# A graph network of four layers on one core: keys loaded and counted first, key and value products inside the first edge sort, zero fill in two halves

## The reference

```python
edge_index = jnp.stack([src, dst])
x = _layernorm(x + _L0(x, edge_index, edge_attr_32, Wq, Wk, Wv, We))
x = _layernorm(x + _L1(x, src, dst, kernel, bias))
x = _layernorm(x + _L2(x, edge_attr_64, edge_index, W_node, W_edge, a_node, a_edge))
x = _layernorm(x + _L3(x, node_vec, W_homo, b_homo, W_hete, b_hete, W_self, b_self, src, dst))

# _L0: attention over the edges into each node, 8 heads of 16
scores = einsum('ehc,ehc->eh', q[dst], k[src]) / sqrt(16) + edge_attr @ We.T
alpha = segment_softmax(scores, dst)
out = segment_sum(v[src] * alpha, dst)
```

## Time and profile before

| | us |
|---|---|
| time, median of 3 runs | 3610.65 (3607.81 to 3611.58) |
| time of the profiled execution | 3604.32 |
| span of the profiled execution | 3602.3 |
| TensorE busy | 1759.1 (49%) |
| VectorE busy | 2287.1 (63%) |
| ScalarE busy | 831.7 (23%) |
| GpSimd busy | 1605.7 (45%) |
| mean granted TensorE clock | 0.704 |

### The profile page before, as it was taken

The page is one execution under the profiler, slowest core; times in us unless marked ns, Lnnn a source line. Parts: engine busy times, 40 slices in busy tenths (PEclk is TensorE's granted clock), DMA queues, the critical chain, the costliest instruction groups (busy, mean ns, idle before and its releaser), DMA issues. The chain is left out here.

```text
span 3602.3 us, 41432 instructions
## 1 busy us (share of the span) xinstructions
PE 1759.1 (49%) x11225; PEld 1197.1 (33%) x11225; DVE 2287.1 (63%) x4545; ACT 831.7 (23%) x2162; POOL 1605.7 (45%) x1514
## 2 busy tenths in 40 slices
PE   2301110103256565539971455249301889984994
PEld 1200000002133333327761345224201227863663
DVE  6974444428866666568977555340485995665987
ACT  0220000002222222214541000000101884542331
POOL 0027777730177777717756577600484003530000
PEclk7555555555576767569985787579655999985997
DMA  1944444470588778787740455338094655641861
GB/s 33 412 132 106 105 104 106 105 52 3 161 236 237 234 237 235 224 60 137 159 89 1 100 109 109 40 124 303 31 390 151 234 182 108 129 88 58 223 186 44
DMA packets 685207, 520.38 MB, mean 144 GB/s; under 512 B 396219, under 2 KB 641677, under 8 KB 670935
## 3 DMA queue, kind: packets, MB, share of 16 engines
q1 hardware_dynamic: 626245, 415.27, 45.8%
q0 software_dynamic: 58752, 102.49, 8.2%
HBM read 356.87 MB, written 160.71 MB: 144 GB/s over the span
## 5 line engine op out<-in xcount | busy, mean ns | idle before, releaser
L654 POOL DMA_INDIRECT table<-pay_own,stage x432 | 420.9, 974 | 571.1 <-ACT q L672 237.5
L971 POOL DMA_INDIRECT adjacency<-gm_slot,slot_tmp x440 | 480.6, 1092 | 225.7 <-issue 134.1
L654 POOL DMA_INDIRECT table<-q,stage x424 | 412.2, 972 | 129.2 <-issue 121.9
L633 PE MATMUL banks<-work,acc 128*128 128x52 bf16 x856 | 98.8, 216 | 757.2 <-DVE acc L620 666.0
L633 PEld LDWEIGHTS banks<-work,acc 128*128 128x128 bf16 x856 | 75.1, 116 | 812.6 <-DVE acc L612 561.2
L715 PE MATMUL banks<-pool,both 128*128 x1320 | 269.0, 377 | 25.2 <-issue 20.7
L1981 POOL TENSOR_TENSOR pool<-pool,raw 128x260 f32<-128x260 f32 x110 | 115.1, 1046 | 355.1 <-DMA pool<-table 246.0
L610 DVE TENSOR_SCALAR acc<-acc,pidx 128x512 bf16<-128x512 bf16 x214 | 80.6, 377 | 285.1 <-DMA acc<-low_rows_by_src 277.4
L612 DVE SCALAR_TENSOR_TENSOR acc<-acc,raw,after 128x128 bf16<-128x128 bf16 x856 | 243.0, 344 | 0.0
L1186 PE MATMUL banks<-both,pool 128*128 128x128 f32 x880 | 157.4, 342 | 131.5 <-DVE both L1517 131.4
L715 PEld LDWEIGHTS banks<-pool,both 128*128 128x128 bf16 x1320 | 163.9, 124 | 100.3 <-issue 42.2
(11 more groups left out here) (462 smaller groups left out, 4413.3 us busy)
## 6 DMA issues: line engine op xcount, KB each, us to landing
work<-adjacency SPq DMA_DIRECT2D x75, 1600.0 KB, 6.7
adjacency<-slots SPq DMA_DIRECT2D x30, 1320.0 KB, 33.0
acc<-table SPq DMA_DIRECT2D x110, 332.0 KB
pool<-table SPq DMA_DIRECT2D x110, 256.0 KB
pool<-table SPq DMA_DIRECT2D x220, 128.0 KB, 2.4
work<-adjacency SPq DMA_DIRECT2D x25, 832.0 KB, 5.4
work<-adjacency SPq DMA_DIRECT2D x25, 768.0 KB, 5.0
acc<-low_rows_by_dst SPq DMA_DIRECT2D x110, 128.0 KB, 4.4
```

What stands on the lines that cost most here:

```text
L633: nc.tensor.matmul(to, rohT_keys[k % 2][:, j, :], pairs[o][:, :, bass.ds(n * G + j, 1), :] .rearrange("p h t s -> p h (t s)"), start=True, ...
L654: nc.gpsimd.indirect_dma_start(to, bass.IndirectOffsetOnAxis(ap=stage[k][:, j:j + 1], axis=0), pay[k][:, j, 0:width], None).then_inc(lande ...
L971: nc.gpsimd.indirect_dma_start(adjacency, bass.IndirectOffsetOnAxis(ap=pair_at[:, t:t + 1], axis=0), pair_n[:, t:t + 1], None).then_inc(co ...
```

## The change

- The two edge key arrays are loaded ahead of the node features, ahead of SyncE's wait for the clearing of `xs`, and VectorE splits them in the start block. The block no longer waits for the weights; TensorE does, ahead of its first transpose in the first sort.
- The key and value products and their split go into the first sort as seven more entries of its pipeline (`key_value_parts`), with work at every fourth step, one block of nodes at a time. ACT makes the high and the middle part, VectorE the two subtractions.
- The folding of the attention vectors, and the split of the node vector (25 columns), go into the block between the sorts.
- The zero fill is cut in two: 16 pieces in the first counting as before, and the remaining 15, with the two fills of 440 KB, in the block between the sorts, behind the five number loads on SyncE's stream. The wait for them moves to `slot_ids`.

```diff
@@ -272,11 +272,14 @@
-        s_w, s_c, s_cd, s_wp = sem("weights_loaded"), sem("iotas_ready"), sem("consts_chain"), sem("wfold_done")
-        s_xz = sem("x_cleared")
+        s_w, s_c, s_xz = sem("weights_loaded"), sem("iotas_ready"), sem("x_cleared")
+        s_kl, s_kc = sem("keys_loaded"), sem("keys_chain")
+        ints = [slot_tmp[k][:, 0:ET].bitcast(I32) for k in range(4)]
         with nc.Block() as block:
...
             def _(sp):
+                for k in range(2):
+                    sp.dma_start(ints[k], keys[k]).then_inc(s_kl, 16)
                 sp.wait_ge(s_xz, 1)
@@ -299,7 +302,6 @@
...
                     sp.dma_start(b3[:, j, :], L3_b[j:j + 1, :].to_broadcast([P, D])).then_inc(s_w, 16)
-                sp.wait_ge(s_w, 16 * 21)
@@ -327,21 +329,15 @@
...
                 nc.vector.tensor_scalar(pidx[:, :], diff[:, 0:1], -1.0, None, ALU.mult)
-                ch = Chain(v, s_cd)
-                v.wait_ge(s_w, 16 * 21)
-                ch.link(nc.vector.tensor_copy(a_rep, avec[:, 3:4].to_broadcast([FE64, P])))
-                v.wait_ge(s_wp, 2)
-                nc.vector.tensor_copy(wge[:, :], ps[0][:, 0:FE64])
-
-                nc.vector.tensor_copy(wn[:, 64:65], ps[1][:, 1:2])
-                nc.vector.tensor_copy(wn[:, 65:66], ps[1][:, 0:1])
-                nc.vector.tensor_copy(wn[:, 66:67], ps[1][:, 2:3])
-
-            @block.tensor
-            def _(pe):
-                pe.wait_ge(s_cd, 1)
-                nc.tensor.matmul(ps[0][:, 0:FE64], a_rep, wedge[:, :], start=True, stop=True).then_inc(s_wp, 1)
-                nc.tensor.matmul(ps[1][:, 0:4], wnode[:, :], avec[:, :], start=True, stop=True).then_inc(s_wp, 1)
+                ch = Chain(v, s_kc)
+                v.wait_ge(s_kl, 32)
+                for k in range(2):
+                    ch.link(nc.vector.tensor_scalar(ints[2 + k], ints[k], 7, None, ALU.arith_shift_right))
+                    ch.link(nc.vector.tensor_scalar(ints[k], ints[k], P - 1, None, ALU.bitwise_and))
+                for k in range(2):
+                    nc.vector.tensor_copy(raw[:, 2 * k, 0:ET], ints[k])
+                    nc.vector.tensor_scalar(raw[:, 2 * k + 1, 0:ET], ints[2 + k], 1.0, None, ALU.add)
+                nc.vector.memset(work[:, 0:NH * (ET + 1)].rearrange("p (h t) -> p h t", h=NH)[:, :, 0:1], 0.0)
@@ -855,6 +851,7 @@
...
                     ch = Chain(v, s_sl)
+                    v.wait_ge(s_az, 16 * CLEARS)
                     tmp = slot_tmp[0][:, :]
@@ -1310,54 +1307,85 @@
-        node_products("kv", lambda b: xs[:, b, :], 2 * D, wqkv[:, D:3 * D], take_kv)
-        s_kp, s_kl, s_kc = sem("kv_parts"), sem("keys_loaded"), sem("keys_chain")
-        ints = [slot_tmp[k][:, 0:ET].bitcast(I32) for k in range(4)]
-        with nc.Block() as block:
-            @block.sync
-            def _(sp):
-                for k in range(2):
-                    sp.dma_start(ints[k], keys[k]).then_inc(s_kl, 16)
-
-            @block.vector
-            def _(v):
-                split16(Chain(v, s_kp).link, kv_rest, [kv16[:, :, k, :] for k in range(3)])
-                ch = Chain(v, s_kc)
-                v.wait_ge(s_kl, 32)
-                for k in range(2):
-                    ch.link(nc.vector.tensor_scalar(ints[2 + k], ints[k], 7, None, ALU.arith_shift_right))
-                    ch.link(nc.vector.tensor_scalar(ints[k], ints[k], P - 1, None, ALU.bitwise_and))
-                for k in range(2):
-                    nc.vector.tensor_copy(raw[:, 2 * k, 0:ET], ints[k])
-                    nc.vector.tensor_scalar(raw[:, 2 * k + 1, 0:ET], ints[2 + k], 1.0, None, ALU.add)
-                nc.vector.memset(table["src"][:, :, 0:1], 0.0)
+        def key_value_parts():
+
+            s_t, s_c, s_p, s_h, s_r, s_m, s_l = (sem(f"kv_{k}") for k in (
+                "turned", "turned_copied", "product", "high_kept", "rest_left", "middle_kept", "low_kept"))
+            rest = [own_row[k][:, :, :].rearrange("p g n -> p (g n)").bitcast(F32) for k in range(2)]
+            product = ps[1][:, 0:2 * D]
+
+            def each_block(todo):
+                return lambda eng, n, k: todo(eng, n // 4) if n % 4 == 0 and n // 4 < NB else None
+
+            def turn(pe, b):
+                if b == 0:
+                    pe.wait_ge(s_w, 16 * 21)
+                wait(pe, s_c, b)
+                nc.tensor.transpose(ps[0][:, 0:P], xs[:, b, :], ident[:, :]).then_inc(s_t, 1)
+
+            def copy(act, b):
+                act.wait_ge(s_t, b + 1)
+                wait(act, s_p, b - 1)
+                nc.scalar.copy(xt[:, b % 2, :], ps[0][:, 0:P]).then_inc(s_c, 1)
+
+            def multiply(pe, b):
+                pe.wait_ge(s_c, b + 1)
+                wait(pe, s_r, b)
+                nc.tensor.matmul(product, xt[:, b % 2, :], wqkv[:, D:3 * D], start=True, stop=True).then_inc(s_p, 1)
+
+            def high(act, b):
+                act.wait_ge(s_p, b + 1)
+                nc.scalar.copy(kv16[:, b, 0, 1:KVW], product).then_inc(s_h, 1)
+
+            def left(v, b):
+                v.wait_ge(s_h, b + 1)
+                wait(v, s_l, b - 1)
+                nc.vector.tensor_tensor(rest[b % 2], product, kv16[:, b, 0, 1:KVW], ALU.subtract).then_inc(s_r, 1)
+
+            def middle(act, b):
+                act.wait_ge(s_r, b + 1)
+                nc.scalar.copy(kv16[:, b, 1, 1:KVW], rest[b % 2]).then_inc(s_m, 1)
+
+            def low(v, b):
+                v.wait_ge(s_m, b + 1)
+                nc.vector.tensor_tensor(kv16[:, b, 2, 1:KVW], rest[b % 2], kv16[:, b, 1, 1:KVW], ALU.subtract).then_inc(s_l, 1)
+
+            return {"tensor": [(2, each_block(multiply)), (0, each_block(turn))],
+                    "scalar": [(5, each_block(middle)), (3, each_block(high)), (1, each_block(copy))],
+                    "vector": [(6, each_block(low)), (4, each_block(left))]}
+
         s_az = lasting_sem("adjacency_cleared")
-        def clear_adjacency(sp):
+        def clear_fills(sp):
...
                              slots[:, 0:2, :].rearrange("p k t -> p (k t)")).then_inc(s_az, 16)
+
+        def clear_adjacency(sp, first, last):
+
             cells = adjacency[0:CELLS, :].rearrange("(p n) o -> p (n o)", p=P)
-            for c in range(CLEARS - 2):
+            for c in range(first, last):
                 n = min(6 * T, CELLS // P - c * 6 * T)
...
         counting = histogram("src")
-        counting["sync"] = {"begin": clear_adjacency, "step": [lambda sp, i: None], "steps": ET // (2 * G)}
+        counting["sync"] = {"begin": lambda sp: clear_adjacency(sp, 0, CLEARS // 2), "step": [lambda sp, i: None], "steps": ET // (2 * G)}
         run((counting, 0, ET // (2 * G), 1))
...
         loads, parts, ready = own_rows()
-        run((stepwise("src", together(placing, parts, scatter_rows("src", loads, table1, ROW1, ready, placing["placed"])),
+        run((stepwise("src", together(placing, parts, scatter_rows("src", loads, table1, ROW1, ready, placing["placed"]),
+                                      key_value_parts()),
                       cleared), 0, ET // (4 * G), 1), lead=T)
...
         s_rb = [sem(f"sorted_ids_loaded{c}") for c in range(5)]
+        s_cd, s_wp = sem("fold_chain"), sem("fold_products")
         back = pay_own[:, :, :, :].rearrange("p k g n -> p (k g n)")[:, 0:4 * T].rearrange("p (t c) -> p t c", c=4)
@@ -1367,11 +1395,29 @@
...
                                      .rearrange("(t p) c -> p t c", p=P)).then_inc(s_rb[c], 16)
+                clear_adjacency(sp, CLEARS // 2, CLEARS - 2)
+                clear_fills(sp)
...
             def _(v):
-                v.wait_ge(s_az, 16 * CLEARS)
                 nc.vector.memset(table["dst"][:, :, 0:1], 0.0)
+                ch = Chain(v, s_cd)
+                ch.link(nc.vector.tensor_copy(a_rep, avec[:, 3:4].to_broadcast([FE64, P])))
+                rest = small[:, 0, 0:NB]
+                ch.link(nc.vector.tensor_copy(rest, nv[:, :]))
+                split16(ch.link, rest, [kv16[:, :, k, 0] for k in range(3)])
+                v.wait_ge(s_wp, 2)
+                nc.vector.tensor_copy(wge[:, :], ps[0][:, 0:FE64])
+
+                nc.vector.tensor_copy(wn[:, 64:65], ps[1][:, 1:2])
+                nc.vector.tensor_copy(wn[:, 65:66], ps[1][:, 0:1])
+                nc.vector.tensor_copy(wn[:, 66:67], ps[1][:, 2:3])
+
+            @block.tensor
+            def _(pe):
+                pe.wait_ge(s_cd, 1)
+                nc.tensor.matmul(ps[0][:, 0:FE64], a_rep, wedge[:, :], start=True, stop=True).then_inc(s_wp, 1)
+                nc.tensor.matmul(ps[1][:, 0:4], wnode[:, :], avec[:, :], start=True, stop=True).then_inc(s_wp, 1)
         counting = histogram("dst")
```

## The result

| | before | changed |
|---|---|---|
| time, median (range), 4 runs each | 3609.23 us (3606.98 to 3611.58) | 3580.34 us (3573.31 to 3582.76) |
| ratio to before, 95% interval | | 0.9917 (0.990 to 0.9934) |
| span of the profiled execution | 3602.3 us | 3571.5 us |
| mean granted TensorE clock | 0.704 | 0.832 |
| counting starts | 89.92 us | 30.51 us |

The kernel got 28.9 us faster, 0.8%. From the page of the changed kernel: the span, busy times, and two rows of the 40 slices, the granted clock and the DMA share. The clock is at 0.9 and above in the first ten slices, 893 us, where it was 0.50 in counting and first sort before.

A forecast was written before the change was run, and what follows sets the result against it. No one engine bounds the kernel: a plain sequence at the start, then VectorE (counting), GpSimd (first sort), SyncE's issues between the sorts. -59.9 + 1 + 0 + 30.4 = -28.5 us gives 3582 us, range 3568 to 3602.

The forecast's parts named there:

- part 1: Start, products and split: keys load early, the block no longer waits for weights, counting starts at 30.06 instead of 89.92: -59.9 us.
- part 2: Products and split inside the first sort: waits are covered, only VectorE's operations slow GpSimd's scatters a little: +1 us.
- part 3: Fold and small split between the sorts: about 3 us of work hidden under VectorE's 26.10 idle us: 0.
- part 4: Second half of the fill between the sorts: the block ends with SyncE's last issue, 827.8 instead of 797.42: +30.4 us.
- slower: Rival, first sort: the new stages' chain of ACT and VectorE uses up the lead, GpSimd waits: 127 us, 3709; chance 0.04.
- lock: Rival, first sort: each VectorE subtraction blocks GpSimd for its length: +20 us, 3602, or 3592 if only two-SBUF-input ones; chance 0.10.
- the trace bears it out little: First sort, against the skill's port lock: scatters keep 965 ns beside four two-input VectorE operations per group (line 612).
- My estimate for TensorE (0.9 us per pass): First sort: 432 ns per product pass doubled for a granted clock of 0.50, 45 us beside 476 idle.
- 28 us of work left in the queue: Between the sorts: SyncE's last fill issue ends when the DMA queue still holds 28 us of work, at 827.8.
- the low bound, SyncE's own pace: Between the sorts: 14 fills at 1.25 us each and three small ones at a third of it take 19 us.
- Issue pace: Rival, between the sorts: SyncE never meets a full queue, so +19 us instead of +30.4, 3571; chance 0.12.
- full drain: Rival, between the sorts: SyncE gets free only when all fills have landed, +58.4 us, 3610, no change; chance 0.06.

The follow-up runs named there:

- experiment 5: The changed kernel itself run once more, on a second chip: 3587.57 us, ratio to the kernel before 0.993.
- 1 to 3: Changed kernel with all fills in the first counting (3556.50 us), the second half in the five countings (3552.36 us), or eight fills between the sorts (3570.81 us).
- experiments 1 and 2: Changed kernel with all zero fills in the first counting (3556.50 us), and with their second half inside the five countings behind the read-back block (3552.36 us).
- Experiment 12: Changed kernel with products and split again a stage of their own ahead of the counting, one run: 4210.05 us, 1.003 times the kernel before.

## Why the prediction was right, and where its terms were off

The forecast was 3582 with -28.5 us, measured were 3580.3 and -28.9. That close an agreement was luck: the terms are off by more, and what made up for them was not in the sum. By stages, from starts in the two profiles:

| step | predicted | measured |
|---|---|---|
| part 1, start to counting | -59.9 | 30.51 - 89.92 = -59.4 |
| part 2, first sort | +1 | 530.8 - 527.8 = +3.0 (+2.8 in experiment 5, +3.9 to +4.4 in 1 to 3) |
| part 3, fold between the sorts | 0 | 0 (VectorE idles 56.84 us there) |
| part 4, fills between the sorts | +30.4 | 64.93 - 32.35 = +32.6 |
| up to the first copy of the read-back | -28.5 | 774.08 - 797.87 = -23.8 |
| all behind it | 0 | -7.0 in the first profile |

**Part 1** holds in mechanism and size. SyncE's last issue comes 0.47 us later than before (24.36 instead of 23.89); from there to the counting it is 4.71 us, against 3.93 + 0.8 in the sum.

**Part 2** holds in its cover: no wait of the new stages reaches GpSimd, and *slower* (the chain) is ruled out by the idle time above, which stays its own issue. The size was off by 2 us, and the term that failed is the price for VectorE's work on the scatters. I took it from means of the second sort, where a product with two inputs from SBUF runs in each group, as a small price on every scatter. In fact a scatter that starts during such an operation is held to its end, and few do. The gaps between the scatters add up to 126.5 us before and after; beyond 958 ns each, the scatters took 3.75 us in all before and 6.69 after, which is the whole of the 3.0 us. Per scatter that meets the low step it is 0.09 to 0.20 us in the mean, 2.2 to 4.9 us for 25. The operand's place decides: in PSUM it is 0.02 to 0.04, and a scatter that starts during the step does not wait.

So *lock* was right in its mechanism and wrong in its count: it had every step holding GpSimd up, 10 or 20 us. The Trainium skill's rule in SBUF — State Buffer, "SBUF: two separate sides", has VectorE with two SBUF inputs lock GpSimd out for the whole instruction; the trace agrees, with 42 of 42 scatters that started during a low step held to its end. The sentence in the prediction that the trace bears it out little rested on the mean of 965 ns and was a misreading. In the kernel before, 30 scatters start at least 0.08 us into an operation of line 612 that has at least 0.13 us left. All 30 end 0.83 to 0.84 us after that operation does, and last 969 to 1097 ns, against 958 for most others.

My estimate for TensorE (0.9 us per pass) was too high: a pass took 714 ns, at a granted clock of 1.00 where I had counted on 0.50, and there was cover for either. From the groups by line in the first sort:

```profile
L1334 PE MATMUL banks<-wqkv,xt 128*128 128x256 f32 x50 | 30.5, 714 | 61.5 <-ACT xt L1329 61.5
...
L1351 DVE TENSOR_TENSOR pool<-acc,pool 128x256 bf16<-128x256 f32 x25 | 10.4, 418 | 0.0
```

**Part 4** holds in mechanism: the border waits for SyncE's last issue, and experiments 1 and 2 show that nothing else costs. The term "28 us of work left in the queue" was mis-sized, and in its unit. The zeros were all down at 799.2 us, 58.2 us behind the last number load's issue, as the 58.4 of the sum has it; but 25.6 us of that were left at the last issue's end, and not 28. I counted bytes, so the three small transfers at the end should have been cheap; in fact each takes as long as a large one, 1.25 us free or 2.8 held, since what holds an issue is ten transfers that have not landed. What I had as the low bound, SyncE's own pace, also missed that the first fill waits for the number load ahead of it, 6.6 us. The rule that fits is 6.6 + 0.5, then 1.25 each up to 13 transfers, then 2.8 to 3.1: 7.1 + 11 x 1.25 + 11.5 = 32.4, measured 32.6. *Issue pace* and *full drain* are both out. The Trainium skill's Perfetto Trace Analysis, "DMA Instruction — HWDGE (DVE, Sync)", has the engines begin before an issue ends, particularly if more descriptors are made than fit in the descriptor buffer. No run here shows that buffer; the count of ten is read from the landings alone.

**Behind the first copy of the read-back** I had nothing, and the first profile shows 7 us less. Of it 5.5 lie in the score pass, a stage whose length goes from 250.5 to 260.5 between executions of these kernels. On the second chip the changed kernel is 26.6 us below the kernel before (0.993). Both intervals, 24 to 36 us and 19 to 31, reach the 23.8 that the stages show. So two terms were too small by 4.2 us together, part 1 won 0.5 less, and the spread of another stage made up for it. What the other microseconds of the first median are stays open; no profile shows them in a stage that the change touches.

The thing that the prediction saw and did not follow to its end: half of the win was given back at a border that the fills need not have stood at.

## What to carry to other kernels

Where an engine's stream in a stage only issues transfers, the end of the stage is when it has issued the last one. Ask of every transfer that is moved which border waits for its issue, not only whether its data is hidden: the same 20 MB cost 32.7 us in a block with nothing else as long, and nothing in the blocks before and behind it. Count such issues by their number and by what stands ahead of them. And beside GpSimd's scatters look at single scatters, not at their mean: one that starts while VectorE has both inputs in SBUF waits to the end of that operation, and with one input in PSUM it does not.

## What the runs showed of the hardware that I had not expected

**The granted clock stayed up and bought nothing.** Before the change TensorE ran the products without a break (busy 14.0 of the 14 us from 33 to 47, at a granted clock of 1.00), and the granted clock fell behind them to 0.50, the 1.2 GHz level, up to the second sort. In the changed kernel, where no such stretch is, it stayed at 1.00, 2.4 GHz, through counting and first sort. Experiment 12 has the stretch again and the fall behind it (length, busy PE, PEld, DVE, ACT, POOL, clock):

```profile
28.00:46.00 18.00, 15.79 (x66) 11.63 (x67) 9.73 (x41) 7.02 (x23) 0.00 (x0) 1.00 0.00 1
...
60.00:87.00 27.00, 1.08 (x4) 0.69 (x4) 23.48 (x5) 0.91 (x4) 0.00 (x0) 0.50 0.01 4
90.00:170.00 80.00, 28.91 (x408) 18.83 (x408) 79.06 (x204) 26.39 (x102) 0.00 (x0) 0.50 0.64 263
```

Counting and first sort were no shorter at the higher level: 81.9 us for 81.8, with TensorE busy 29.45 us for 29.51. And a float32 pass inside the sort took 714 ns at a granted 1.00, where the packed stage before had a mean of 432, at a granted 1.00 as well. The granted clock of a stretch by itself does not tell how long a sparse matmul takes.

**A small transfer is held as long as a large one.** 2.79 and 2.81 us for 440 KB, 3.08 for 1320 KB, 1.25 for either where nothing is held. In the changed kernel and in the kernel before, the issues began to be held when ten earlier fills had not landed, and not at nine.

**A scatter waits for the rest of a VectorE operation with two SBUF inputs, and the other way round.** Where the scatter came first, VectorE's operation gets longer: in the kernel before, those of line 612 that started 0.02 to 0.08 us ahead of a scatter ended 0.32 us into it in 28 cases of 31, whenever they had started, so that one lasted up to 0.40 us instead of 0.35. Operations with one input in PSUM (line 620) held no scatter there, in 39 cases of 39. The masks of line 610, with one bf16 tensor from SBUF, held 16 of 17.

**One kernel on four chips:** 3609, 3614, 4195 and 4198 us, with stalls of TensorE's stream of up to 17.9 us on the latter two.
